# Edge sums and maxima over quads of edges, and edge counts by gathers, in a graph network block

## The reference

```python
h = relu(layernorm(x))
out1 = segment_sum(edge_attr, dst)                  # 96
cnt  = segment_sum(1, dst)
out2 = where(cnt > 0, segment_max(edge_attr, dst), 0)
out3 = out1 / max(cnt, 1)
f = concat([h, out1, out2, out3, u[0]])             # 256 + 3 * 96 + 64
x = x + relu(f @ W1 + b1) @ W2 + b2 + h
h = relu(layernorm(x))
x = x + gat2(elu(gat1(h)))                          # attention over edges and self loops
```

## Time and profile before

| | us |
|---|---|
| median of 3 runs (lowest to highest) | 6095.52 (6086.31 to 6099.28) |
| the profiled execution, its own time | 6058.5 |
| its span | 6056.1 |

### The profile page before, as it was taken

One profiled execution on the slowest core, in us unless ns is written; L12 is line 12 of the kernel. 1 busy time (PEld: TensorE's weight loads), 2 busy tenths in 40 slices (PEclk: granted clock), 3 DMA queues, 4 the chain that ended last, 5 costly groups with the idle time before them and its releaser, 6 DMA issues. The chain is left out here.

```text
span 6056.1 us, 34007 instructions
## 1 busy us (share of the span) xinstructions
PE 1486.5 (25%) x7221; PEld 1212.5 (20%) x7221; DVE 4633.5 (77%) x8166; ACT 3138.9 (52%) x2827; POOL 3860.8 (64%) x3935
## 2 busy tenths in 40 slices
PE   5677799999300000000000006300000000000000
PEld 4556588888200000000000004200000000000000
DVE  8999677777588788878887866477777777777765
ACT  7996222222255555555555544355565556555640
POOL 1321244444477777777777757777777777777756
PEclk9999899999655555555555557655555555555555
DMA  9999534333366666666666655366666666666659
GB/s 335 373 370 377 198 128 125 119 126 123 119 215 211 213 224 215 211 215 223 215 211 215 223 178 172 101 223 219 211 211 223 219 211 211 223 219 211 211 202 308
DMA packets 359089, 1292.02 MB, mean 213 GB/s; under 512 B 83249, under 2 KB 175473, under 8 KB 328849
## 3 DMA queue, kind: packets, MB, share of 16 engines
q1 hardware_dynamic: 168560, 761.20, 33.6%
q0 software_dynamic: 180320, 476.50, 26.9%
q10 hardware_dynamic: 10048, 52.70, 2.1%
HBM read 681.57 MB, written 608.52 MB: 213 GB/s over the span
## 5 line engine op out<-in xcount | busy, mean ns | idle before, releaser
L169 POOL DMA_INDIRECT rows<-table_d,k_src x3128 | 2981.9, 953 | 984.7 <-issue 952.6
L222 ACT ACTIVATE rows<-totals 128x1472 f32<-128x1472 f32 (+2 forms) x560 | 2068.1, 3738 | 1218.9 <-DVE totals L325 1218.3
L325 DVE TENSOR_TENSOR_SCAN totals<-mask,turned 128x1536 f32<-128x1536 f32 (+2 forms) x560 | 1796.1, 3249 | 0.0
L187 PE MATMUL pB<-diag,k_ones 128*128 128x512 f32 (+1 forms) x4 | 2.9, 822 | 4002.6 <-DVE diag L351 4002.6
L315 DVE TENSOR_TENSOR turned<-rows,pT 128x1472 f32<-128x1472 f32 (+2 forms) x560 | 918.4, 1640 | 0.0
L187 PEld LDWEIGHTS pB<-diag,k_ones 128*128 128x128 f32 x4 | 1.0, 313 | 4003.3 <-DVE diag L351 4003.3
L276 DVE TENSOR_TENSOR z<-rows,ad 128x92 f32<-128x92 f32 (+3 forms) x140 | 30.8, 220 | 791.9 <-DMA rows<-table_d,k_src 791.9
L989 POOL DMA_INDIRECT k_lone_ea<-in_ea,k_gather x196 | 206.5, 1053 | 481.7 <-DVE mid_feat L1340 351.3
L746 PE MATMUL pH<-hT_pre,w1h 128*128 128x256 f32 x1568 | 412.7, 420 | 137.3 <-ACT hT_pre L621 123.5
L746 PEld LDWEIGHTS pH<-hT_pre,w1h 128*128 128x128 f32 x1568 | 322.0, 212 | 213.1 <-ACT hT_pre L621 141.8
L1228 PE MATMUL pM<-w,hid 128*128 128x256 f32 x1568 | 360.9, 383 | 2.7 <-issue 2.2
(11 more groups left out here) (249 smaller groups left out, 3563.8 us busy)
## 6 DMA issues: line engine op xcount, KB each, us to landing
sums_d<-rows SPq DMA_DIRECT2D x134, 3036.0 KB, 10.6
ea<-in_ea SPq DMA_DIRECT2D x98, 768.0 KB, 8.8
rows_d<-run SPq DMA_DIRECT2D x97, 768.0 KB, 7.4
pre_d<-pre ACTq DMA_DIRECT2D x49, 1024.0 KB, 8.9
pre_in<-pre_d SPq DMA_DIRECT2D x49, 1024.0 KB, 4.9
rows<-table_d,k_src POOLq DMA_INDIRECT x3128, 2.8
hrow_c<-table_d SPq DMA_DIRECT2D x98, 256.0 KB, 4.5
table_d<-g_rows SPq DMA_DIRECT2D x49, 264.0 KB, 3.1
```

What stands on the lines that cost most here:

```text
L169: p.indirect_dma_start(out=rows[:, g.slot, k, :], out_offset=None, in_=table, in_offset=bass.IndirectOffsetOnAxis(ap=keep["src"][:, e:e + ...
L222: ins = a.activation(rows[:, g.slot, 0:g.size, q * PD:(q + 1) * PD], laid(totals[:, q, :], g.size)[:, :, 1:].rearrange("p d k -> p k d"), ...
L325: v.tensor_tensor_scan(totals[:, q, 0:n], mask[:, g.n % 2, 0:n], turned[q % 2][:, 0:n], 0.0, ALU.mult, ALU.add).then_inc(summed, 1)
```

## The change

Edges are chained in quads: after the pair step two more tensor_tensors join pairs into quads (4 per group), and the chain has one step per quad, 8 instructions per group in place of 16. The stored rows halve. A node's total now lacks up to three edges at either end. GpSimd gathers the whole quad before and the whole quad behind (1536 bytes a row), and the node stage masks six edges of these (`lone` has six columns per node tile), reduces them and adds the chained row: two tensor_tensors, two reduces and two tensor_tensors per step. The scaling of the features stays on VectorE as it was.

The counts no longer come from ScalarE. The 1568 last destinations of the tiles are given as a table `dst_last` of 32 blocks of 49 (KB, BB; a further input). VectorE compares each node with the tops of the 32 blocks (`nearest_blocks`, before the first group), GpSimd gathers the block of 49 per node (`lasts_of_block`), and `whole_tiles` counts in it. The loads, copies and products that spread `last_i` are gone. The fixed group numbers become 8 b + 6 for whole_tiles and six groups later for edges_of_tile.

```diff
-    GB = G // 2
-    BW = EW // 2
-    BLOCKS = s.EP // 2
+    GB, GQ = G // 2, G // 4
+    QW = EW // 4
+    BLOCKS = s.EP // 4
+    KB, BB = io["dst_last"].shape
...
-        def counted_by(b):
-
-            return -(-JB * (b + 1) // COUNTS) - 1
-
-        FULL_AT = {PAIR * counted_by(b) + 6: b for b in range(NBL)}
-        EDGES_AT = {g + 7: b for g, b in FULL_AT.items()}
+        FULL_AT = {8 * b + 6: b for b in range(NBL)}
+        EDGES_AT = {g + 6: b for g, b in FULL_AT.items()}
...
-            def count_tiles(n):
-                for j in range(COUNTS * n, min(COUNTS * n + COUNTS, NT)):
-                    if j:
-                        a.wait_ge(counted_act, j)
-                    a.activation(junk_act[:, :], last_all[:, :], ACT.Sign, bias=node_above[:, j:j + 1], scale=-1.0,
-                                 accum_out=signs[:, j:j + 1]).then_inc(counted_act, 1)
-
-            a.dma_start(last_i[:, :], io["dst"].rearrange("(t e) -> t e", e=P)[:, P - 1:P]
-                        .rearrange("t e -> e t"), allow_slow_non_contiguous=True).then_inc(last_in, 16)
+            a.dma_start(tops_i[:, :], io["dst_last"][:, BB - 1:BB].rearrange("k o -> o k").to_broadcast([P, KB]),
+                        allow_slow_non_contiguous=True).then_inc(last_in, 16)
             a.wait_ge(masked, 9)
...
-            g.wait_ge(last_in, 16)
-            g.tensor_copy(last_f[:, :], last_i[:, :]).then_inc(last_ready, 1)
             tiles_of = lambda name: io[name].rearrange("(t e) -> t e", e=P)
+
+            def lasts_of_block(b):
+                g.wait_ge(near_ready, b + 1)
+                if b >= 2:
+                    g.wait_ge(lasts_used, b - 1)
+                for q in range(JB):
+                    g.indirect_dma_start(
+                        out=lasts[:, b % 2, q, :], out_offset=None, in_=io["dst_last"],
+                        in_offset=bass.IndirectOffsetOnAxis(ap=near_i[:, b * JB + q:b * JB + q + 1], axis=0),
+                    ).then_inc(lasts_in[b % 2], 16)
+
+            for b in range(min(2, NBL)):
+                lasts_of_block(b)
...
+                if b + 2 < NBL:
+                    lasts_of_block(b + 2)
...
+            link = Chain(v, joined)
+            link(v.tensor_tensor(joins[:, 1:QW], same[:, 1:EW - 6:4], same[:, 2:EW - 5:4], ALU.mult))
+            link(v.tensor_tensor(joins[:, 1:QW], joins[:, 1:QW], same[:, 3:EW - 4:4], ALU.mult))
+            link(v.tensor_tensor(uniform[:, :], same[:, EW - 3:EW - 2], same[:, EW - 2:EW - 1], ALU.mult))
+            link(v.tensor_tensor(uniform[:, :], uniform[:, :], same[:, EW - 1:EW], ALU.mult))
+            v.tensor_tensor(joins[:, 1:QW], joins[:, 1:QW], same[:, 4:EW - 3:4], ALU.mult).then_inc(masked, 1)
...
+            def nearest_blocks():
+                v.wait_ge(last_in, 16)
+                v.wait_ge(nodes_ready, 1)
+                for b in range(NBL):
+                    js = slice(b * JB, (b + 1) * JB)
+                    done(v.tensor_tensor(le[:, :, 0:KB], tops_i[:, :].unsqueeze(1).to_broadcast([P, JB, KB]),
+                                         node[:, js].unsqueeze(2).to_broadcast([P, JB, KB]), ALU.is_le))
+                    done(v.tensor_reduce(near[:, js], le[:, :, 0:KB], AX.X, ALU.add))
+                    v.tensor_copy(near_i[:, js], near[:, js]).then_inc(near_ready, 1)
+
             def whole_tiles(b):
                 js = slice(b * JB, (b + 1) * JB)
-                v.wait_ge(counted_act, JB * (b + 1))
-                v.tensor_scalar(full_i[:, js], signs[:, js], 0.5, ET / 2, ALU.mult, ALU.add).then_inc(full_ready, 1)
+                v.wait_ge(lasts_in[b % 2], 16 * JB * (b // 2 + 1))
+                v.tensor_tensor(le[:, :, 0:BB], lasts[:, b % 2, :, :], node[:, js].unsqueeze(2).to_broadcast([P, JB, BB]),
+                                ALU.is_le).then_inc(lasts_used, 1)
+                v.wait_ge(lasts_used, b + 1)
+                done(v.tensor_reduce(inner[:, js], le[:, :, 0:BB], AX.X, ALU.add))
+                v.scalar_tensor_tensor(out=full_i[:, js], in0=near[:, js], scalar=float(BB), in1=inner[:, js],
+                                       op0=ALU.mult, op1=ALU.add).then_inc(full_ready, 1)
...
+                done(v.tensor_scalar(half_i[:, 0, :], half_i[:, 0, :], 3, None, ALU.add))
+                done(v.tensor_scalar(half_i[:, :, :], half_i[:, :, :], 2, None, ALU.arith_shift_right))
+                done(v.tensor_copy(half[:, :, :], half_i[:, :, :]))
+                done(v.tensor_scalar(keep["gather"][:, 1, :], half[:, 0, :], -1.0, 0.0, ALU.add, ALU.max))
+                done(v.tensor_scalar(keep["gather"][:, 3, :], half[:, 1, :], float(BLOCKS - 1), None, ALU.min))
...
+                for i in range(1, 4):
+                    done(v.tensor_scalar(lone[:, 0, :, i - 1], ahead, float(4 - i), None, ALU.is_ge))
+                    done(v.scalar_tensor_tensor(out=lone[:, 0, :, i - 1], in0=left, scalar=float(i - 4),
+                                                in1=lone[:, 0, :, i - 1], op0=ALU.is_gt, op1=ALU.mult))
+                    done(v.tensor_scalar(lone[:, 0, :, i + 2], behind, float(i - 1), None, ALU.is_gt))
+                done(v.tensor_scalar(lone[:, 1, :, :], lone[:, 0, :, :], -1.0, BIG, ALU.add, ALU.mult))
...
-            def pairs_of_edges(g):
+            def quads_of_edges(g):
                 v.wait_ge(ea_in[g % BUFS], 16 * (g // BUFS + 1))
                 if g >= 2:
-                    v.wait_ge(chained, 2 * GB * (g - 1))
-                for m, op in enumerate((ALU.add, ALU.max)):
+                    v.wait_ge(quaded, 2 * (g - 1))
+                kinds = (ALU.add, ALU.max)
+                for m, op in enumerate(kinds):
                     v.tensor_tensor(duo[:, g % 2, m, :, :], ea[:, g % BUFS, 0:G:2, :], ea[:, g % BUFS, 1:G:2, :],
                                     op).then_inc(paired, 1)
-
-            pairs_of_edges(0)
-            for e in range(BW):
-                g, k = e // GB, e % GB
+                if g >= 2:
+                    v.wait_ge(chained, 2 * GQ * (g - 1))
+                for m, op in enumerate(kinds):
+                    v.wait_ge(paired, 2 * g + m + 1)
+                    v.tensor_tensor(quad[:, g % 2, m, :, :], duo[:, g % 2, m, 0:GB:2, :], duo[:, g % 2, m, 1:GB:2, :],
+                                    op).then_inc(quaded, 1)
+
+            nearest_blocks()
...
+            quads_of_edges(0)
+            for e in range(QW):
+                g, k = e // GQ, e % GQ
                 if k == 0:
                     between(g)
...
-                    before = begin[:, m, :] if e == 0 else run[:, (e - 1) // GB % BUFS, (e - 1) % GB, m, :]
+                    before = begin[:, m, :] if e == 0 else run[:, (e - 1) // GQ % BUFS, (e - 1) % GQ, m, :]
                     if e:
                         v.wait_ge(chained, 2 * e + m - 1)
                     v.scalar_tensor_tensor(out=run[:, g % BUFS, k, m, :], in0=before, scalar=by[:, e:e + 1],
-                                           in1=duo[:, g % 2, m, k, :], op0=op0, op1=op1).then_inc(chained, 1)
+                                           in1=quad[:, g % 2, m, k, :], op0=op0, op1=op1).then_inc(chained, 1)
...
-def gather_lone_edges(g, io, keep, n, landed):
-
+def gather_end_quads(g, io, keep, n, landed):
+
+    quads = io["ea"].rearrange("(q k) f -> q (k f)", k=4)
     for t in range(2):
         for i in range(2):
             g.indirect_dma_start(
-                out=keep["lone_ea"][:, n % 2, t, i, :], out_offset=None, in_=io["ea"],
-                in_offset=bass.IndirectOffsetOnAxis(ap=keep["gather"][:, 1 + i, 2 * n + t:2 * n + t + 1], axis=0),
+                out=keep["lone_ea"][:, n % 2, t, 4 * i:4 * i + 4, :].rearrange("p k f -> p (k f)"), out_offset=None, in_=quads,
+                in_offset=bass.IndirectOffsetOnAxis(ap=keep["gather"][:, 1 + 2 * i, 2 * n + t:2 * n + t + 1], axis=0),
...
-                lone = lambda i, j: keep["lone"][:, i, bass.ds(j, 1)]
                 kinds = ((ALU.mult, ALU.add), (ALU.add, ALU.max))
-                for t in range(2):
-                    for m, (op0, op1) in enumerate(kinds):
-                        v.scalar_tensor_tensor(out=mid[:, 0, t, m, :], in0=lone_ea[:, at.par, t, 0, :],
-                                               scalar=lone(2 * m, at.n * 2 + t), in1=agg[:, at.par, t, m * EF:(m + 1) * EF],
-                                               op0=op0, op1=op1).then_inc(mids, 1)
-                for t in range(2):
-                    for m, (op0, op1) in enumerate(kinds):
-                        v.wait_ge(mids, at.n * 8 + (2 * t + m + 1))
-                        v.scalar_tensor_tensor(out=mid[:, 1, t, m, :], in0=lone_ea[:, at.par, t, 1, :],
-                                               scalar=lone(2 * m + 1, at.n * 2 + t), in1=mid[:, 0, t, m, :],
-                                               op0=op0, op1=op1).then_inc(mids, 1)
+                base = at.n * 6
+                for m, (op0, _) in enumerate(kinds):
```

(43 more changed lines are left out.)

82 lines of the change are left out of this document (38 added, 44 removed).

## The result

The changed kernel takes 6118.5 us (median of 8 runs, 6105.9 to 6127.0) against 6093.9 before: 1.0050 times as long, 95% interval 1.0029 to 1.0071. The forecast was 6127. The total agrees, but its two large terms don't: the loss of 21 us forecast for the edge chain isn't there, and the node stage loses 69 us where 10 were forecast.

A forecast was written before the change was run, and what follows sets the result against it. VectorE was taken to bound the edge chain (ScalarE and DMA close behind), TensorE the node stage. Edge chain +21 and node stage +10 gave +31 on the median 6095.5: 6127 us, range 6045 to 6200.

The forecast's parts named there:

- The chain: Edge chain: eight chain instructions fewer, two 384-element tensor_tensors more; net -0.89 us a group over 98 groups, -87 us.
- The start: Before the first edge group: waiting for block tops, then nearest_blocks, moves it from 15.7 to 50.5 us; +24.6 us.
- the lower end: Start of edge chain: tops land as fast as 1568 single words did, at 25.6 us; 40 was taken.
- the upper end: Start of edge chain: tops land in proportion to their 4096 words, at 62.5 us, 22 us more in the sum.
- The gathers: Edge chain: GpSimd's 196 gathers, held by long tensor_tensors, pass two per group at 2.33 us each; VectorE waits +77 us.
- rival 1: Edge chain: GpSimd keeps up, no gathers held, the 77 us of waits goes; total 6049 us; chance 0.21.
- nothing for that: Edge chain: DMA engines carry no more per microsecond, 0.82 of the bytes in 0.84 of the time; no charge.
- Counting leaves ScalarE: Edge chain: 98 ScalarE passes of 1.60 us go; VectorE's waits for ScalarE's roots lose their later part, -11.5 us.
- Node stage: Node stage: VectorE's extra 3.75 us a step covered by its waits; +6 for unevenness, +4 for first call, +10 us.
- the upper end of 0.5 more: Node stage: each reduce over groups of six costs up to 0.5 us above the price taken.
- rival 3: Node stage: VectorE bounds it if reduces cost 0.5 us more, steps grow by 1.0; +47, 6174 us; chance 0.12.
- Rival 4: Edge chain: 106 us of gather waits or tops at 62; +52 to +60, 6150 to 6187 us; chance 0.13.

The follow-up runs named there:

- own rows: Changed kernel, but the table of last nodes copied 128 times in HBM, each partition's gathers reading its own copy; 6065.6 us (0.9985 of before).
- both edits: Changed kernel with 128 table copies, one per partition, and three tensor_tensors per kind replacing the node stage's reduction; 6009.0 us (0.9894 of before).
- lower group: Kernel before, unchanged: its runs near 6053 us, mean granted clock 0.629; the profile before (6058.5 us) is of these.
- The second experiment: Changed kernel with masked edges written so that a group's six values lie side by side and the reduction reads contiguously; 6118.6 us (one execution).
- upper group: Kernel before, unchanged: its runs near 6088 us, mean granted clock 0.619; seven of its eight runs in the result are of these.

## Why the prediction was right in sum and wrong in its parts

*The chain* (-87): right. Groups are 4.51 and 4.78 us apart where nothing waits, 4.65 on average as forecast; the quad tensor_tensor takes 0.47 to the next instruction.

*The start* (+24.6): the tops landed at the lower end, 21.4 us after their issue:

```profile
24.18 0.63 DVE L799 TENSOR_TENSOR le<-tops_i,node 128x448 bf16<-128x448 int32 x1 [9.08 <-DMA tops_i<-in_dst_last]
33.91 1.82 DVE L932 TENSOR_TENSOR duo<-ea 128x768 f32<-128x768 f32 x2
```

33.9 - 15.7 - 12.2 = 6 us. The 4096 words landed no later than the 1568 of the earlier trace rows; the Trainium skill's rule of one descriptor per element (DMA: Bandwidth & Descriptors, Rules for kernel authors), which spoke for the upper end, does not give the time here. whole_tiles (2.1 us each) and nearest_blocks (9.7) were right.

*The gathers* (+77): wrong twice. In the changed kernel VectorE stood so often for edges that the gathers, at 1.29 us each, were in time. But with own rows, where it hardly stands, the wait is 17.3 us, near rival 1 (nothing) and far from the two gathers per group of the forecast. Timeline of that kernel, GpSimd and VectorE's pair steps:

```profile
38.84 1.82 DVE L940 TENSOR_TENSOR duo<-ea 128x768 f32<-128x768 f32 x2
39.08 1.52 POOL L674 DMA_INDIRECT lasts_e<-last_d,near_i  x1 [0.30 <-issue]
40.91 1.03 POOL L674 DMA_INDIRECT lasts_e<-last_d,near_i  x1 [0.30 <-issue]
42.25 0.94 POOL L674 DMA_INDIRECT lasts_e<-last_d,near_i  x1 [0.31 <-issue]
43.42 1.82 DVE L940 TENSOR_TENSOR duo<-ea 128x768 f32<-128x768 f32 x2
43.49 3.50 POOL L674 DMA_INDIRECT lasts_e<-last_d,near_i  x1 [0.30 <-issue]
...
48.19 1.82 DVE L940 TENSOR_TENSOR duo<-ea 128x768 f32<-128x768 f32 x2
48.68 1.28 POOL L674 DMA_INDIRECT lasts_e<-last_d,near_i  x1 [0.30 <-issue]
```

The gather that begins 0.07 us into a pair step is held for 3.50 us; those that begin 0.24 and 0.49 into one pass in 1.52 and 1.28. In the kernel with both edits, 24 of 196 gathers begin within an eighth of a us of a pair step's start and take 3.0 us on average, 15 begin 0.4 to 0.6 us into it and take 1.3. So by these rows it is a part of a gather that collides. The forecast held every gather that met a step; on average they cost 1.33 us (1427 and 1226 ns) and a gap of 0.30, not 2.33. (What held the one at 126.45 in the earlier trace rows, which began 1.09 us ahead of its step, stays open.) The Trainium skill's rule (SBUF — State Buffer, Who interferes with whom) agrees in that such pairs collide, but does not give how seldom; the same section's report that tensor_tensor was not seen to stall descriptor writing, which spoke for rival 1, is not what the gather of 3.50 us shows.

*DMA* ("nothing for that"): the step that failed in the edge chain. The forecast counted bytes, and these did fall. It gave the 98 new gathers their issue on GpSimd and no time on the DMA engines, where q0 holds 46.6% of all 16 in the stretch shown. That cost 72 us of waits (60.7 and 11.0), by chance the size of the 77 forecast for another reason; but the end of the chain, with the start 19 us cheaper, came at 632 and not 651.

*Counting leaves ScalarE* (-11.5): right in the lower group; in the upper one it is worth 33 us more (56.0 - 22.9).

*Node stage* (+10): the step that failed, and the mis-sized term, is the reduction: 0.87 + 384 x 1.04 = 1.27 us was taken, 2.07 each (4.15 for two) is what it takes, outside the upper end of 0.5 more. The rest of the group was right: the multiplications follow each other at 1.27, VectorE's three waits did cover 3.75 us, and of the 2 x 0.80 us on top the step shown has 1.24 (where the other 0.36 went was not traced). From the first multiplication to that of the last step the stage is 69 us longer: 12 in its first three steps, 5 in one in the middle and 51 in the other 44. This is the mechanism of rival 3 with a larger price. Both rows that the price rested on read contiguous groups; the new one reads at a stride of 96 elements, which the diff shows and the working never asked. The Trainium skill has the rule (SBUF — State Buffer, Door 1: The DMA port swizzle): consecutive accesses within one 16-byte line run at full rate, and each that crosses to a new line pays. The second experiment agrees: 2.15 us at a stride of 384 bytes, 1.34 without.

*Rival 4*: its terms, 29 us more waits or 22 us later tops, make 6155 or 6148, and both 6177; the 6187 that it names is not their sum. This touched neither the forecast nor its range.

So 31 us were forecast over the profiled execution's 6058.5, as +21 and +10; 66 came in the spans, as -2, +69 and -1.5. That the time was hit all the same is luck: the 31 were added to a median of the upper group, 37 us above the profiled execution, and the change took that group's loss of 35 us away, which the sum did not have. The two misses, 35 us too little and 37 too much, cancel.

## What to carry to other kernels

Price an instruction by a row with the same access pattern, not only the same count: here 1152 fp32 elements cost 1.34 us contiguous and 2.15 to 2.23 strided, and three contiguous tensor_tensors were cheaper than one strided reduction. An indexed gather whose partitions all want the same few rows cost DMA-engine time far beyond its bytes here; a copy of the small table for each partition, or for each sixteen, took that away. When a stage has no slack and two limits close behind, look at DMA busy share beside GB/s: a full share at a fallen rate (0.95 at 265 GB/s, after 1.00 at 385) was the mark of dear packets.

## What the runs showed of the hardware that was not expected

- Reads of the same 196-byte rows of HBM by all 128 partitions: 390 packets of the gathers' queue took 119 of 256 engine-us in a 16 us stretch (306 ns each); with a row for each partition 296 packets took 15 (51 ns each). Over 30 to 560 us, a packet of eight such rows took 851 ns, 129 with 128 copies of the table and 101 with eight.
- TensorE, waiting 3.28 to 4.5 us in every turn of the same program, had a mean granted clock of 0.91 in one execution and of 0.77 in another over the same 430 us.
- VectorE pays nearly the same for a strided fp32 read and a strided write: 1.34 us became 2.15 (stride of 384 bytes) and 1.35 became 2.23 (24 bytes) for 1152 elements.
- An indexed gather of GpSimd that began within an eighth of a us of the start of a pair of two-input tensor_tensors took 3.0 us on average, one that began 0.4 to 0.6 us into the pair 1.3, and a free one 0.95.
